# A decoder of twelve stages: two of four token batches of each mixture routed inside the attention stage ahead of it, one of them scattered there

## The reference, cut to what matters

```python
def _L1_ffn_ref(x, gate_w, gate_b, sh_w1, ...):          # the mixture "f1"
    router_probs = softmax(einsum('bsd,de->bse', x, gate_w) + gate_b)
    expert_values, expert_indices = top_k(router_probs, k=2)
    expert_values = expert_values / (sum(expert_values) + 1e-09)
    h = gelu(einsum('bsd,edi->bsei', x, ew1) + eb1)
    all_outputs = einsum('bsei,eid->bsed', h, ew2) + eb2
    moe_out = einsum('bse,bsed->bsd', weights_E, all_outputs)
    return x + _mlp(x, sh_w1, sh_b1, sh_w2, sh_b2) + moe_out

def _L3_ffn_ref(hidden_states, wr, w1, b1, w2, b2):      # the mixture "f3"
    vals, idx = top_k(x @ wr.T, 2)
    gating = softmax(vals of the two)
    pos = cumsum(mask, axis=0) - 1        # place of a token in its expert's list
    keep = mask & (pos < cap)             # cap = 1280
    y = gelu(xg @ w1 + b1) @ w2 + b2      # per expert, on the tokens gathered
    return segment_sum(y * g, ...)        # back to the tokens
```

## Time and profile before

| | |
|---|---|
| device time, three runs | 2322.65 to 2328.99 us, median 2326.48 |
| profiled execution | 2327.09 us; its span, first to last instruction, 2325.2 us |
| mean granted TensorE clock | 0.864 of full |
| busy in the span | PE 1763.3 us (76%), PEld 1214.8 (52%), DVE 1321.2 (57%), ACT 1103.7 (47%), POOL 746.2 (32%) |
| L2766, the scatter into `slots` | 128 indirect DMAs, 124.6 us of POOL, 960 to 970 ns each |
| L2773, the scatter into `back` | 158 indirect DMAs, 151.7 us of POOL |

### The profile page before, as it was taken

The page is one execution under the profiler, slowest core; times in us unless marked ns, Lnnn a source line. Parts: engine busy times, 40 slices in busy tenths (PEclk is TensorE's granted clock), DMA queues, the critical chain, the costliest instruction groups (busy, mean ns, idle before and its releaser), DMA issues. The chain is left out here.

```text
span 2325.2 us, 39403 instructions
## 1 busy us (share of the span) xinstructions
PE 1763.3 (76%) x14513; PEld 1214.8 (52%) x14513; DVE 1321.2 (57%) x3525; ACT 1103.7 (47%) x2265; POOL 746.2 (32%) x713
## 2 busy tenths in 40 slices
PE   3887561799996996859996685887788868751994
PEld 1555441545553664646896452655555535451774
DVE  2888578512235774563343465885379979851223
ACT  3676440333345776723442243773357657610431
POOL 1223200271364321057354002331223232156453
PEclk9888795699997998968998686999879969955997
DMA  4111272036624101112576001000000010011224
GB/s 154 83 82 83 90 241 69 15 104 168 181 54 171 78 2 47 28 40 99 172 234 206 10 1 33 24 20 10 3 1 2 2 37 29 11 45 66 69 77 139
DMA packets 143730, 173.19 MB, mean 74 GB/s; under 512 B 20913, under 2 KB 118897, under 8 KB 142609
## 3 DMA queue, kind: packets, MB, share of 16 engines
q1 hardware_dynamic: 123956, 129.09, 18.0%
q0 software_dynamic: 13248, 28.21, 3.6%
q10 hardware_dynamic: 6336, 13.37, 1.5%
HBM read 126.84 MB, written 79.05 MB: 89 GB/s over the span
## 5 line engine op out<-in xcount | busy, mean ns | idle before, releaser
L2773 POOL DMA_INDIRECT f_back<-f_ys,f_row x158 | 151.7, 960 | 175.8 <-DVE f_ys L2934 146.6
L2766 POOL DMA_INDIRECT f_slots<-f_pay,f_slot x128 | 124.6, 973 | 66.0 <-issue 38.1
L874 PE MATMUL a_AV<-a_vx,a_pT 128*64 128x18 f32 (+1 forms) x3072 | 115.1, 224 | 33.0 <-DVE a_two L544 15.3
L874 PEld LDWEIGHTS a_AV<-a_vx,a_pT 128*64 128x64 f32 x3072 | 105.9, 146 | 62.2 <-issue 28.6
L736 ACT ACTIVATE a_e<-a_e 128x512 f32<-128x512 f32 x192 | 110.2, 622 | 59.0 <-DVE a_e L566 58.9
L861 PE MATMUL a_TP<-ident,a_e 128*128 128x128 f32 x768 | 108.0, 285 | 19.9 <-ACT a_e L736 19.3
L741 ACT COPY a_pT<-a_TP 128x512 f32<-128x512 f32 x192 | 103.5, 588 | 39.5 <-PE a_TP L861 39.4
L861 PEld LDWEIGHTS a_TP<-ident,a_e 128*128 128x128 f32 x768 | 89.2, 146 | 57.5 <-ACT a_e L736 48.3
L566 DVE TENSOR_TENSOR a_e<-a_S,a_mx 128x1024 f32<-128x1024 f32 x96 | 117.3, 1222 | 2.9
L850 PE MATMUL a_S<-a_kbd,a_qT 64*64 64x512 f32 x768 | 114.2, 670 | 1.0 <-issue 0.6
L3000 ACT ACTIVATE f_h<-f_H,f_wt 128x256 f32<-128x256 f32 x156 | 67.1, 474 | 81.2 <-PE f_H L3096 81.2
(11 more groups left out here) (481 smaller groups left out, 4573.3 us busy)
## 6 DMA issues: line engine op xcount, KB each, us to landing
f_wt<-in_f_ew SPq DMA_DIRECT2D x39, 584.0 KB
f_slots<-in_blank SPq DMA_DIRECT2D x1, 18576.0 KB
f_wt<-in_f_leaf SPq DMA_DIRECT2D x94, 98.0 KB, 2.0
f_pay<-f_back SPq DMA_DIRECT2D x8, 1024.0 KB, 8.1
f_xs<-f_slots SPq DMA_DIRECT2D x47, 144.0 KB
memory_x_k<-w_stage ACTq DMA_DIRECT2D x24, 256.0 KB, 3.1
f_slots<-in_blank SPq DMA_DIRECT2D x1, 5760.0 KB
f_xs<-leaf_slots SPq DMA_DIRECT2D x22, 256.0 KB, 3.3
```

The lines of the kernel that those rows point to most:

```text
L874: last = pe.matmul(AV[64 * c:64 * c + 64, 2 * hp * W1:2 * (hp + 1) * W1], pT[:, hp, 64 * c:64 * c + 64], vx[:, g % 2, t, c, 2 * hp:2 * hp ...
L2766: pool.indirect_dma_start(out=slots[:, :], out_offset=bass.IndirectOffsetOnAxis(ap=slot[:, c, t:t + 1], axis=0), in_=pay[:, c, t, :], in_o ...
L2773: pool.indirect_dma_start(out=back[:, :], out_offset=bass.IndirectOffsetOnAxis(ap=row[:, i % RR, t:t + 1], axis=0), in_=ys[:, i % RY, t, : ...
```

## The change

A class `Router` takes over what `routed` did for a batch, with the same operations. Its memory is opened ahead of the attention and lives to the end of the mixture. `routed` becomes `mixture`. Batches 0 and 1 (the first 16 tiles) are now normalised, routed and placed between the tiles of the attention, batch 0 is scattered by POOL at the end of its list there; batches 2 and 3 are routed in the mixture, which scatters batches 1, 2 and 3. The matrices `tri`, `ones`, `sel` and `before` become bf16, so that `place` runs on bf16 operands. In `f1` the shared expert starts at once, and the loads of the router and of the shared weights move into the attention. `pay` is split into two halves, one of them (`payA`) in `k.f0w` for `f3`. The core of the diff:

```diff
 # attention(), for x3
+    begun = {2 * b + 2: b for b in range(r.AHEAD)} if r else {}
 # SP: r.load(sp) ahead of the loads of keys and values. POOL:
+                if g in begun:
+                    r.root(pool, begun[g])
...
+            if r:
+                r.scatter(pool, 0)
 # DVE, after each tile
+            def route(g, t):
+                if t == 1 and g in begun:
+                    v.wait_ge(x_updated.sem, x_updated.after(g - 1))
+                    r.norm_stats(v, begun[g])
+                if t == 3 and g in begun:
+                    for j in range(r.BT // 2):
+                        r.scale(v, begun[g], j)
+                if t == 0 and g - 1 in begun:
...
+                if t == 1 and g - 2 in begun:
+                    r.take_logits(v, begun[g - 2], no_fill)
+                if t == 2 and g - 2 in begun:
+                    r.pick(v, begun[g - 2], no_fill)
+                if t == 3 and g - 2 in begun:
+                    r.weigh(v, begun[g - 2])
+                if t == 0 and g - 3 in begun:
+                    r.give_slots(v, begun[g - 3])
 # memory_attention(), x1: batch = {2: 0, 4: 1}
 # SP
+            r.load(sp)
+            WR = d["f1_sh"].shape[1]
+            sp.dma_start(k.f0w[:, NB * SL:NB * SL + WR], d["f1_sh"]).then_inc(k.shared_in, 16)
 # DVE
             v.wait_ge(cleared.sem, 1)
+            r.begin(v)
             for i in steps:
                 if within(i):
                     shift(i)
+                if i - 3 in batch:
+                    r.give_slots(v, batch[i - 3])
...
                 if within(i - 1):
                     take_values(i - 1)
+                if i in batch:
+                    v.wait_ge(x_updated.sem, x_updated.after(i - 1))
+                    r.norm_stats(v, batch[i])
+                if i - 2 in batch:
+                    r.take_logits(v, batch[i - 2], no_fill)
...
                     weigh_features(i + 2)
+                if i in batch:
+                    for j in range(r.BT):
+                        r.scale(v, batch[i], j)
+                if i - 2 in batch:
+                    r.make_shares(v, batch[i - 2], no_fill)
+                    r.pick(v, batch[i - 2], no_fill)
+                    r.weigh(v, batch[i - 2])
 # ACT
             for i in steps:
+                if i - 2 in batch:
+                    r.take_turned(act, batch[i - 2], 0)
+                    r.take_turned(act, batch[i - 2], 1)
                 if within(i - 1):
                     take_weights(i - 1)
...
                     open_gate(i + 1)
+                if i - 2 in batch:
+                    r.gaps(act, batch[i - 2])
+                    r.copy_rows(act, batch[i - 2])
 # mixture(), POOL
-            root(0)
-            root(1)
-            root(2)
...
+            r.pad(pool, payB[:, :])
+            r.root(pool, 2)
+            r.scatter(pool, 1)
+            r.root(pool, 3)
+            r.scatter(pool, 2)
+            r.scatter(pool, 3)
 # mixture(), DVE
+            choose(2, lambda j: r.scale(v, 3, j))
```

More of the change, by code:

```diff
@@ L1908, in memory_attention @@
     PJ, TP, AV, S = ph.ps("PJ", [P, 2, 512]), ph.ps("TP", [P, 2, 512]), ph.ps("AV", [P, 2, 512]), ph.ps("S", [P, GT, 2, SL])
+    RT = ph.ps("RT", [P, 512])
+    r.banks(lambda n: RT[:, :] if n else PJ[:, 1, :], RT[:, :], RT[:, :])
+    batch = {GT * b // 2 + 2: b for b in range(r.AHEAD)}
     setup_in, cleared = ph.counter("setup_in"), ph.counter("cleared")
@@ L1949, in _ @@
                                    k.neghalf[:, 0:2 * GT], ALU.pow).then_inc(root_ready.sem, 1)
+                if g == 0:
+                    r.prepare(pool)
+                if g - 4 in (0, 2):
+                    r.root(pool, (g - 4) // 2)
+            r.scatter(pool, 0)
         @block.vector
@@ L2166, in _ @@
                     score(i)
+                if i - 3 in batch:
+                    r.place(pe, batch[i - 3])
+                if i - 2 in batch:
+                    r.make_logits(pe, batch[i - 2])
                 if within(i - 1):
@@ L2169, in _ @@
                 if within(i + 1):
+                    if i - 2 in batch:
+                        pe.wait_ge(r.xT_ready.sem, r.xT_ready.after(batch[i - 2], 1))
                     turn(i + 1)
@@ L2175, in _ @@
                     make_gate(i + 1)
+                if i - 1 in batch:
+                    b = batch[i - 1]
+                    r.turn_x(pe, b, 0, (products_taken.sem, products_taken.after(i + 1)))
+                    r.turn_x(pe, b, 1, (r.places_taken.sem, r.places_taken.after(b - 1)) if b else None)
     ph.close()
@@ L2945, in _, with take_batch @@
                 v.wait_ge(back_in[b].sem, 16)
-                link(v.tensor_tensor(xb, xb, got[:, BT * b:BT * b + BT, 0:P], ALU.add))
-                v.tensor_tensor(xb, xb, got[:, BT * b:BT * b + BT, P:2 * P], ALU.add).then_inc(x_added.sem, 1)
+                link(v.tensor_tensor(xb, xb, got(b)[:, :, 0:P], ALU.add))
+                v.tensor_tensor(xb, xb, got(b)[:, :, P:2 * P], ALU.add).then_inc(x_added.sem, 1)
         @block.scalar
         def _(act):
-            def copy_rows(b):
-                act.copy(pay[:, 1, BT * b:BT * b + BT, 0:P], pay[:, 0, BT * b:BT * b + BT, 0:P]).then_inc(copied.sem, 1)
-            def take_turned(b):
-                for n in range(2):
-                    act.wait_ge(x_turned.sem, x_turned.after(b, n + 1))
-                    if b and not shared:
-                        act.wait_ge(logits.sem, logits.after(b - 1))
-                    act.copy(xTall[:, 2 * b + n if shared else n, :], PJ[:, n, :]).then_inc(xT_ready.sem, 1)
-            def gaps(b):
-                s = slice(BT * b, BT * b + BT)
-                act.wait_ge(gap_ready.sem, gap_ready.after(b))
-                if shared:
-                    act.activation(pe_[:, s, :], pe_[:, s, :], ACT.Exp).then_inc(e2_ready.sem, 1)
-                else:
-                    act.activation(e2[:, s], gap[:, s], ACT.Exp).then_inc(e2_ready.sem, 1)
+            def take_batch(b):
+                r.take_turned(act, b, 0)
+                r.take_turned(act, b, 1)
+                r.copy_rows(act, b)
             def shared_gelu(n):
@@ L3054, in yield_shared @@
                 last.then_inc(sh_out.sem, 1)
-            pe.wait_ge(setup_in.sem, n_early)
-            turn_x(0)
-            make_logits(0)
             if shared:
-                pe.wait_ge(late_in.sem, n_late)
-            for b in range(NBAT):
-                if b + 1 < NBAT:
-                    turn_x(b + 1)
-                place(b)
-                if b + 1 < NBAT:
-                    make_logits(b + 1)
-                elif shared:
-                    pe.wait_ge(ones_made.sem, ones_made.after(NBAT))
-                    pe.wait_ge(logits_taken.sem, logits_taken.after(NBAT - 1))
-                    pe.matmul(LG[:, 0:E], ones[:, :], before[:, NBAT, 0, :], start=True, stop=True).then_inc(counted.sem, 1)
-                if shared:
-                    do_shared(b)
-                    yield_shared(b)
-            for n in range(NBAT, NSH):
-                do_shared(n)
-                yield_shared(n)
+                pe.wait_ge(k.shared_in, 16)
+                do_shared(0)
+                yield_shared(0)
+                turn_batch(2)
+                r.make_logits(pe, 2)
+                do_shared(1)
+                yield_shared(1)
+                r.place(pe, 2)
+                turn_batch(3)
+                r.make_logits(pe, 3)
+                do_shared(2)
+                yield_shared(2)
+                r.place(pe, 3)
+                count_all()
+                for n in range(3, NSH):
+                    do_shared(n)
+                    yield_shared(n)
+            else:
+                turn_batch(2)
+                r.make_logits(pe, 2)
+                turn_batch(3)
+                r.place(pe, 2)
+                r.make_logits(pe, 3)
+                r.place(pe, 3)
             def turn(i):
@@ L3284, in decoder, with ahead @@
         load_all(nc, k, d)
+        routers = {}
+        def ahead(tag):
+            routers[tag] = Router(nc, k, d, tag, tag == "f1")
+            return routers[tag]
         phases = {
```

528 lines of the change are left out of this document (330 added, 198 removed).

## The result

| | before | predicted | after |
|---|---|---|---|
| device time, median of 20 runs each | 2327.49 us | 2326.0 | 2334.06 us |
| ratio to before, 95% interval | | 0.9995 (2326.0 to the profiled 2327.09) | 1.0022, 1.0012 to 1.0032 |
| span and mean granted clock of the profiled execution | 2325.2 us, 0.864 | | 2334.7 us, 0.859 |
| `x1`, from POOL's first instruction to DVE's first in `f1` | 109.2 | 140.2 | 145.7 |
| `f1`, from there to PE's first expert block | 121.8 | 97.5 | 94.8 |

What follows compares the result with a forecast made beforehand. It took f3 to be bound by 24.4 us of routing one batch, then 64 scatters in a row, and x1 by a three-engine loop. +31.0 - 24.3 + 23.2 - 31.0 = -1.1 us, as written, gave 2326.0 us; range 2312 to 2342.

Steps and rivals of the forecast that it cites:

- step 4 of `x1`: In x1: ACT's two copies, the logits and half the turned weights precede ACT's copy of those weights; +4.4 us.
- step 6: In x1: the same router work as in step 4 but without statistics; +3.8 us.
- A second term, `x3`: In x3: two batches routed on DVE, 20.4 us, and six earlier loads, 2.8 us; loses 23.2 us (18 to 28).
- the signs that I had named: Wrong if x1 is below 132 or above 148 us, its clock under 0.7, or x3 outside 182 to 193.
- steps 5 and 7: In x1: choice, place and turned weights precede ACT's copy; 10.9 and 5.5 us, with ACT waiting some 6 us each.
- the wait behind the root of batch 3: In f1 and f3: batch 2's choice waits for this root behind 16 scatters; POOL idle 9.6 us in f3.
- the case that I kept in the upper end: In x3: the 16 scatters hold up DVE by 0.84 us each, 13 us; a few kept in the upper bound.
- the sum of this half: x3 and f3 together: f3 gains 31.0 us and x3 loses 23.2; 7.8 us less.
- the rival of the low clock: In x1: PE's added waits bring 1.2 GHz, 17 us more, 2343; decides below clock 0.7; chance 0.20.

Runs made afterwards that it cites:

- first experiment: Changed kernel with batch 3's statistics and root moved ahead of the scatter of batch 1 in both mixtures: 2315.36 us, ratio 0.9953.
- tenth experiment: Changed kernel with 22 unread matmuls on PE between scores and logits of steps 4 and 6 in x1: 2327.65 us, ratio 1.0001.
- eleventh experiment: Only the x3 and f3 half of the change; x1 and f1 as in the kernel before: 2321.45 us, ratio 0.9972.
- the second: Changed kernel with ACT's copies of the router's turned tokens between the halves of its normalisation in x1: 2319.82 us, ratio 0.9961.
- third: Changed kernel with PE counting places behind the weighting of the values in x1, and slots made behind the values: 2334.54 us, ratio 1.0035.
- sixth: Kernel with roots first, mid-normalisation copies and later x3 loads, plus DVE's choice ahead of the values in x1: 2289.80 us, ratio 0.9842.
- eighth: Changed kernel without its bf16 part, matrices, choices and place counts in f32: 2345.65 us, ratio 1.0082.

## Why the prediction was right in size and wrong in sign

In short: the step that failed is step 4 of `x1`, and step 6 with it. I priced them at the high clock, 4.4 and 3.8 us, and they cost 8.1 and 7.2, because PE waits for ACT's late copies and runs at the low clock behind that wait. A second term, `x3`, was 7.5 us too small in the profile. Of the signs that I had named, `x1` at 145.7 us kept within 132 to 148, and `x3` at 195.2 left its 182 to 193. ACT's waits in steps 5 and 7 were 4.4 and 4.1 us, not 6.

**f3: right.** Each step is in the rows, the wait behind the root of batch 3 among them. The gain is 32.6 for 31.0 us. The difference is mainly `place` in bf16, 0.6 us from its first matmul to DVE's slots instead of the 2.0 that I took between nothing and 4.0; the first scatter behind the idle time comes 1.5 us sooner.

**f1: right, with the same term.** 27.0 for 24.3 us. The first experiment shows the wait to be worth 10.7 us here, a part of it clock, and 7.0 in `f3`. In `f3` POOL was idle for 8.1 and gave up 1 to wait for a second set of statistics.

**x3: the loads and DVE's work nearly right, the clock missed.** The loss of 30.7 us is outside my 18 to 28. Loads 3.1 for 2.8 us. The routing 23.7 for 20.4: DVE's busy time rose by 19.6 us for 18.1 (half of `f3`'s 36.13), and four instructions of batch 0's choice took 0.67 to 0.97 us instead of 0.17 to 0.23:

```profile
2005.12 0.67 DVE L414 TENSOR_TENSOR f3r_gap<-f3r_top 128x8 f32<-128x8 f32 x1
...
2005.95 0.94 DVE L418 TENSOR_TENSOR f3r_eq<-f3r_eq,f3r_rev 128x64 f32<-128x64 f32 x1
...
2007.93 0.97 DVE L425 TENSOR_TENSOR f3r_sel<-f3r_oh 128x64 bf16<-128x64 f32 x1
```

They stand beside POOL's spreading of the keys, 2004.73 to 2008.8. Beside the scatters, 2030.9 to 2051, no instruction of the router took over 0.23 us on DVE, so the case that I kept in the upper end (13 us for scatters that hold up DVE) fell. The rule of the Trainium skill (Advanced Engine Details and Errata, VectorE Performance Modes) sets GpSimd's instructions against those of VectorE in a two-port mode. The four here are tensor operations of two inputs beside POOL's tensor operations, and the indirect DMAs held up none, so my use of the rule for the scatters was wrong. The last 3.9 us are the first group at the low clock, for which `x3` had no term. The larger part of the miss goes with the clock: with the same code `x3` lasted 189.5 us in the tenth experiment, where 0.85 was granted and not 0.81, and a loss of 25.0 us is within my bounds. By the eleventh experiment the sum of this half was 6.5 us for 7.8, but with `x3` and `f3` 7.3 and 1.5 us off in its profile that is in part luck.

**x1: the step that failed.** Step 4, as I wrote it, was "ACT's two copies (1.05), the logits on PE (1.9) and the first half of the turned weights (0.55) must be over before ACT can copy those weights", +4.4 with 0.9 for `weigh`. The order was right and the clock wrong. The delay was 8.1 us: the logits took 3.55, the first half of the turned weights about 1.0, and from ACT's copy to DVE's values it was 5.2 instead of 2.8, nearly all at 1.2 GHz. Step 6 missed by 3.4 us in the same way; I had put it at 3.8 us "as step 4 without statistics", for which step 4's own terms give 4.4, so 0.6 us of the miss is a sum that doesn't come out. I had asked whether ACT's copies delay the weights and not when they come: behind ACT's whole normalisation, 4 us after PE had turned the tokens, and PE's idle time in between is what dropped the clock. I had put 1.5 us for it in the whole stage; steps 4 and 6 alone took 7.1, or 6.5 without that slip. This is the rival of the low clock, at a chance of 0.20 and with its sign set wrong: I let it decide below 0.7 in the window, and at 0.77 it cost 7.1 of the 18.5 us that it could. The tenth experiment shows the clock to be a part of its own, worth 2.5 and 3.5 us a round, the second that both parts go with the order of ACT's list.

**Steps 5 and 7: the right size for a wrong reason.** 10.3 and 5.2 us for 10.9 and 5.5. By the third and sixth experiments it was not `place` ahead of the turned weights but the choice on DVE's list. That the size fits is luck. The eighth shows that `place` would have been on the path had it been as long as in f32.

**The sum.** Against the profiles the mixtures came out 4.3 us better and the attentions 13.0 us worse; the runs put the half of `x1` and `f1` at 5 us over my figure. The forecast balanced 55 us of gains against 54 of losses, so an error of a tenth in either decided the sign. That the time fell in the range is in part two misses, in the mixtures and in the attentions, that offset each other.

## What to carry to other kernels

Work moved into a stage that "has room" is paid in that stage's own loop: walk through each engine's list at the new place and ask when its input is copied and what the waiting engine does to its clock. The same work cost 8.1 and 7.2 us a round where ACT's copies stood at the end of its list, and 1.1 and 0.8 us where they stood in the middle. When a step is taken out of a row of DMAs, look at what still stands between them: one root behind 16 scatters held both mixtures, and moving it was worth 17.7 us in the profile.

## What the runs showed of the hardware

- A wait of 3.5 us of PE in an otherwise busy stretch was followed by about 8 us at a granted clock of 0.50, with PE full; the same stretch stayed at 1.00 when the wait was filled with matmuls (tenth experiment).
- `place` of nine matmuls at 1.2 GHz took 3.9 us in f32 and 0.5 in bf16: not half, as the two recorded passes of f32 had led me to take, but a seventh. Why it is so much is not shown.
- Beside indirect DMAs issued by POOL the router's choice on DVE kept to 0.17 to 0.23 us an instruction; beside POOL's tensor operations four of its instructions took 0.67 to 0.97.
- Kernels whose code for a stage is the same differ in it by up to 6.5 us in the profile (`x3` 189.5 to 196.0), and the granted clock of the stage differs with it (0.85 to 0.79; `f1` took 80.5 us at 1.00 and 84.1 at 0.91). A difference of one stage between two traces means little below that, unless the clocks are compared first.
